# Second attention of a two-layer network: score operands in 32-row strips, stacked by TensorE

## What is computed

```
q = rope((x @ Wqa @ Wqb).reshape(b, s, 16, 8))        # 16 heads of 8
k, v = (x @ Wkva @ Wkvb).reshape(b, s, 4, 8, 2)       # 4 groups of heads share k and v
k = rope(k)
scores = einsum('bqhd,bkhd->bhqk', q, k) * 8**-0.5    # causal mask, then softmax
out = einsum('bhqk,bkhd->bqhd', softmax(scores), v) @ Wout + bout
```

## Time and profile before

| | us |
|---|---|
| three runs | 1310.79, 1312.22, 2832.59 |
| median | 1312.22 |
| span of the profiled execution | 1317.5 |
| PE, DVE, ACT busy in it | 1166.7, 1046.4, 776.6 |

### The profile page before, as it was taken

The page is one execution under the profiler, slowest core; times in us unless marked ns, Lnnn a source line. Parts: engine busy times, 40 slices in busy tenths (PEclk is TensorE's granted clock), DMA queues, the critical chain, the costliest instruction groups (busy, mean ns, idle before and its releaser), DMA issues.

```text
span 1317.5 us, 17710 instructions
## 1 busy us (share of the span) xinstructions
PE 1166.7 (89%) x6249; PEld 680.9 (52%) x6249; DVE 1046.4 (79%) x2018; ACT 776.6 (59%) x1151; POOL 43.9 (3%) x45
## 2 busy tenths in 40 slices
PE   3888647999999855779999999999998799999998
PEld 2333333666666512345444443443332688888886
DVE  4699998788888883879899889888851688888885
ACT  1635414899999710135555656566676566666664
POOL 0000020000000040140000000000000000000000
PEclk9898767899999956589999999999999699999999
DMA  5000000000000214551000000000000121111001
GB/s 161 0 0 1 0 24 17 16 17 16 18 14 1 78 35 79 72 78 16 2 2 2 1 1 2 1 1 1 1 1 1 45 102 56 56 56 56 0 1 33
DMA packets 38169, 35.02 MB, mean 27 GB/s; under 512 B 15162, under 2 KB 33530, under 8 KB 36810
## 3 DMA queue, kind: packets, MB, share of 16 engines
q1 hardware_dynamic: 36082, 31.12, 9.0%
q0 software_dynamic: 2016, 2.96, 1.7%
HBM read 30.85 MB, written 3.08 MB: 26 GB/s over the span
## 4 chain that ended last, share of the span: by engine, by line
PE 61%; DVE 26%; ACT 6%; issue 3%; DMA 3%; SPq 1%; DVEq 0%; ACTq 0%
PE ps L822 10%; PE ps L823 10%; PE ps L824 10%; PE ps L983 9%; DVE arena_a L1766 7%; PE ps L927 7%; PE ps L971 6%; DVE arena_b L1472 3%; DVE mv L1377 2%; PE ps L839 1%; ACT arena_b L1222 1%; DMA arena_a<-q_parts 1%; PE ps L693 1%; DMA arena_a<-arena_a 1%; DVE xn L1384 1%
## 5 line engine op out<-in xcount | busy, mean ns | idle before, releaser
L1766 DVE TENSOR_REDUCE arena_a<-ps 128x1 f32<-128x512 f32 (+3 forms) x560 | 344.4, 668 | 73.2 <-PE ps L931 46.3
L1289 ACT ACTIVATE arena_b<-ps 128x1024 f32<-128x1024 f32 (+3 forms) x320 | 274.0, 894 | 191.8 <-PE ps L971 169.6
L822 PE MATMUL ps<-parts 128*128 128x512 f32 x640 | 273.2, 427 | 7.1 <-DVE parts L1688 4.2
L823 PE MATMUL ps<-parts 128*128 128x512 f32 x640 | 251.5, 393 | 0.0
L824 PE MATMUL ps<-parts 128*128 128x512 f32 x640 | 251.2, 392 | 0.0
L927 PE MATMUL ps<-arena_b,arena_a 128*128 128x512 bf16 (+3 forms) x576 | 190.4, 354 | 6.3 <-DVE arena_a L1766 4.9
L971 PE MATMUL ps<-arena_a,arena_b 128*128 128x512 bf16 (+3 forms) x576 | 163.2, 348 | 0.7 <-ACT arena_b L1289 0.3
L983 PE MATMUL ps<-arena_b 128*32 128x512 f32 (+3 forms) x1280 | 151.1, 544 | 2.5 <-DVE arena_b L1754 2.2
L822 PEld LDWEIGHTS ps<-parts 128*128 128x128 f32 x640 | 122.0, 191 | 36.8 <-DVE parts L1688 9.7
L824 PEld LDWEIGHTS ps<-parts 128*128 128x128 f32 x640 | 121.0, 189 | 26.4
L823 PEld LDWEIGHTS ps<-parts 128*128 128x128 f32 x640 | 121.4, 190 | 22.4
(11 more groups left out here) (274 smaller groups left out, 1445.3 us busy)
## 6 DMA issues: line engine op xcount, KB each, us to landing
arena_b<-expert_weights SPq DMA_DIRECT2D x7, 1024.0 KB, 6.7
arena_a<-q_parts SPq DMA_DIRECT2D x18, 128.0 KB
arena_a<-q_parts POOLq DMA_DIRECT2D x18, 128.0 KB, 5.9
wslot<-in_L_ffn_up_w SPq DMA_DIRECT2D x8, 256.0 KB, 3.1
wslot<-in_L_ffn_down_w SPq DMA_DIRECT2D x8, 256.0 KB, 3.3
wslot<-in_L_ffn_w_gate SPq DMA_DIRECT2D x8, 256.0 KB, 2.9
wslot<-in_L_ffn_w_up SPq DMA_DIRECT2D x8, 256.0 KB, 3.4
wslot<-in_L_ffn_w_down SPq DMA_DIRECT2D x8, 256.0 KB, 3.8
```

What stands on the lines that cost most here:

```text
L822: mm(bank, w(0), x(0), start=start, stop=False)
L823: mm(bank, w(0), x(1), start=False, stop=False)
L1289: a(probs[:, s % 2, 2 * pair:2 * pair + 2, off:CW], ps[:, 2 + 2 * pair:4 + 2 * pair, off:CW], ACT.Exp, scale=scale).then_inc(p2_exp, 1)
L1766: v.tensor_reduce(mx[:, n % 2, i:i + fit, t % TPC, u], b[:, 0:fit * w].rearrange("p (h k) -> p h k", k=w), AX_X, ALU.max)\
```

## The change

The parts of q and k become two fp32r parts each instead of three bfloat16 ones. One head takes KROWS = 24 rows (three pairs of parts of 8 features) and two rows for the maximum, and lies in its own strip of 32 rows; `qst` and `kst` hold the four heads of a group in the four strips, `kst` with the same k in each. A score product contracts 24 rows (slots) or 26 rows (steps) of one strip, where it contracted 128 rows.

- The strips are filled by PE: matmuls with 0/1 matrices `spread` (1 MB, loaded by DMA during the routing, copied to fp32r by POOL) take the parts to their rows (`stack_q`, `stack_k`, 32 units of two products), and ACT copies each bank to `qst` or `kst`, for k with a per-partition bias that puts the ones in place. The DRAM tensors, `stack` and both long memsets are gone.
- Wqa @ Wqb and Wkva @ Wkvb are multiplied once, ahead of the expert layer of layer 0 (two transposes, two products, four ACT copies); `queries`, `keys` and `values_all` then start from the normalized x. k of chunk c is computed into its own 32 rows of banks 6 and 7, so rope and split of k are done once for all chunks (`rope_k`); they need their own rope table `ropek`.
- Slots: a chunk's diagonal blocks of one head go into one bank ("diag", four products of 128 columns and one mask product of 512), the blocks below them into two more ("below3", "below12"). An item has 12 such slots where it had 11; all slots are 616 where they were 600, over the same columns. Slots 0 to 24 run ahead of step 0, after all of q, with `stack_k` of chunks 1 to 3 between them.
- `copy_out` moves from DVE to ACT. The reordering copies of the weights and the addition of the output bias move from DVE to POOL.
- The maximum rows are float32 and go to one strip row of each head.

```diff
-    fit = max(1, CW // ((t % TPC + 1) * P)) if u == t // TPC else 1
-    scores += [("scores", n, t, u, i, fit) for i in range(0, HPG, fit)]
+blocks = [("scores", t, u) for t in range(TPC * c, TPC * c + TPC) for u in range(c)]
+blocks += [("diag", 0, 0), ("below3", 0, 0), ("below12", 0, 0)]
+for k, (what, t, u) in enumerate(blocks):
+    scores += [(what, n, t, u, i) for i in range(HPG)]
     if k == 0 and n > 0:
...
     nc.gpsimd.memset(vaug[:, :, :, HD:HD + 1], 1.0).then_inc(vzero, 1)
...
-        stack(pool, c)
...
+    pool.wait_ge(comb_ready, 2)
+    pool.wait_ge(ld_e, 16)
+    g.tensor_copy(spread, eraw).then_inc(spread_ready, 1)
+    pool.wait_ge(ln_xn, 3 * NC)
+    pool.wait_ge(wo1_ready, 1)
+    g.tensor_tensor(xt[:, :, :], xt[:, :, :], bo1[:, :].unsqueeze(1).broadcast_to([P, NT, D]), ALU.add)\
+        .then_inc(bias_ready, 1)
...
+    nc.tensor.transpose(ps[0:QL, 2, 0:P], wqa[:, :], ident[:, :])
+    nc.tensor.transpose(ps[0:KVL, 3, 0:P], wkva[:, :], ident[:, :]).then_inc(wt_tr, 1)
+    pe.wait_ge(wt_ready, 2)
+    pe.wait_ge(wk_ready, 6)
+    mm(ps[:, 2, 0:2 * D], wqaT[:, :], wqb.rearrange("p a d -> p (a d)"), start=True, stop=True)
+    mm(ps[:, 3, 0:3 * G1 * HD], wkvaT[:, :], wkk.rearrange("p a d -> p (a d)"), start=True, stop=True)\
+        .then_inc(wm_mm, 1)
+    pe.wait_ge(wm_ready, 2)
     for c in range(NC):
...
+    def queries(c):
...
+        pe.wait_ge(ln_h, 2 * NC + c + 1)
...
+        if c >= 2:
+            pe.wait_ge(rope_done, 2 * (c - 1))
+        b = 4 - 2 * (c % 2)
+        mm(ps[:, b, :], wq[:, 0, :], rhs(c), start=True, stop=True)
+        mm(ps[:, b + 1, :], wq[:, 1, :], rhs(c), start=True, stop=True).then_inc(q_mm, 1)
...
+    def keys(c):
...
         pe.wait_ge(ln_h, 2 * NC + c + 1)
...
-            last = mm(ps[:, 2, k * 32:(k + 1) * 32], latk[0:KVL, c % 2, k * P:(k + 1) * P], wkk[:, 2, :],
+        mm(ps[32 * c:32 * c + 32, 6, :], wkv[:, 0, :], rhs(c), start=True, stop=True,
+           tile_position=(0, 32 * c))
+        mm(ps[32 * c:32 * c + 32, 7, :], wkv[:, 1, :], rhs(c), start=True, stop=True,
...
+    def values_all():
+        pe.wait_ge(rope_done, 6)
+        for t in range(NT):
+            last = mm(ps[:, 4, t * 32:(t + 1) * 32], hT[:, PAD + t * P:PAD + (t + 1) * P], wkv[:, 2, :],
                       start=True, stop=True)
...
+    def stack_q(c):
+        pe.wait_ge(split_ready, c + 1)
+        if c == 0:
...
+            e = c * G1 + g
+            if e >= 2:
+                pe.wait_ge(stack_ready, e - 1)
+            mm(ps[:, e % 2, :], spread[:, 0, g, 0, :], q2[:, c % 2, 0, :], start=True, stop=False)
+            mm(ps[:, e % 2, :], spread[:, 0, g, 1, :], q2[:, c % 2, 1, :], start=False, stop=True)\
+                .then_inc(stack_mm, 1)
+    def stack_k(c):
...
+        r = slice(32 * c, 32 * c + 32)
+        for g in range(G1):
+            e = NSTACK + c * G1 + g
+            pe.wait_ge(stack_ready, e - 1)
+            mm(ps[:, 2 + e % 2, :], spread[r, 1, g, 0, :], k2[r, 0, :], start=True, stop=False)
+            mm(ps[:, 2 + e % 2, :], spread[r, 1, g, 1, :], k2[r, 1, :], start=False, stop=True)\
+                .then_inc(stack_mm, 1)
...
+                pe.wait_ge(stack_ready, NSTACK + G1 * (c + 1))
...
+            def pairs(at_, tq, k0, kw, stop=True):
+                return mm(b[:, at_:at_ + kw], qst[r, g, tq * P:(tq + 1) * P], kst[r, g, k0:k0 + kw],
+                          start=True, stop=stop, skip_group_check=not stop)
+            if what[0] == "scores":
+                last = pairs(0, t, u * CW, CW)
+            elif what[0] == "below3":
+                last = pairs(0, TPC * c + 3, c * CW, 3 * P)
+            elif what[0] == "below12":
+                pairs(0, TPC * c + 1, c * CW, P)
+                last = pairs(P, TPC * c + 2, c * CW, 2 * P)
+            else:
+                for k in range(TPC):
+                    pairs(k * P, TPC * c + k, c * CW + k * P, P, stop=False)
+                last = mm(b, identb[:, :], maskqk[:, :].unsqueeze(1).broadcast_to([P, TPC, P]),
+                          start=False, stop=True, skip_group_check=True)
         elif what[0] == "maxima":
             pe.wait_ge(nm_ready, what[1] + 1)
-            last = nc.tensor.transpose(b[0:2 * HPG * TPC, 0:P // 2].bitcast(BF16),
...
+            r = slice(32 * i, 32 * i + MROWS)
+            k = kst[r, g, j * P:(j + 1) * P]
+            q = qst[r, g, chunk(c)]
...
+    keys(NC - 1)
+    queries(2)
+    stack_q(0)
+    queries(3)
+    stack_q(1)
+    stack_q(2)
+    values_all()
+    stack_q(3)
+    stack_k(0)
+    for k, what in enumerate(SLOTS[0]):
         slot(what)
-    latents(NC - 1)
-    heads(NC - 1)
-    for what in FIRST[1]:
-        slot(what)
-    pe.wait_ge(v_ready, NC)
...
+    pe.wait_ge(v_ready, 1)
+    pe.wait_ge(stack_ready, 2 * NSTACK)
     for s, (n, j) in enumerate(STEPS):
...
+        if e < NSTACK:
+            a(qst[:, g, chunk(c)], ps[:, e % 2, :], ACT.Copy).then_inc(stack_ready, 1)
+        else:
+            a(kst[:, g, chunk(c)], ps[:, 2 + e % 2, :], ACT.Identity, bias=onerow[:, :])\
+                .then_inc(stack_ready, 1)
+    norm(2)
...
+        stack_copy(e)
+    act.wait_ge(v_mm, 1)
...
+    def copy_out(n, steps):
...
+        act.wait_ge(pv_mm, steps)
+        if n >= 2:
+            act.wait_ge(slot_read, READ["out", n - 2])
+        a(oT[:, n % 2, :], ps[:, 6, :], ACT.Copy).then_inc(o_copy, 1)
...
+    def rope_q(c):
...
+        b, bank = c % 2, 4 - 2 * (c % 2)
+        dve.wait_ge(q_mm, c + 1)
+        v.tensor_tensor(ra[:, b, :], ps[:, bank, :], ropec[:, chunk(c)], ALU.mult).then_inc(rope_done, 1)
+        v.tensor_tensor(rb[:, b, :], ps[:, bank + 1, :], ropes[:, chunk(c)], ALU.mult).then_inc(rope_done, 1)
+        dve.wait_ge(rope_done, 2 * c + 2)
+        chain(v.tensor_tensor(ra[:, b, :], ra[:, b, :], rb[:, b, :], ALU.add))
         if c >= 2:
-            dve.wait_ge(st_qk[b], 32 * (c // 2))
-        step(v.tensor_copy(q3[:, b, 0, :], ra[:, b, :]))
-        step(v.tensor_copy(k3[0:KR, b, 0, :], rk[0:KR, b, :]))
-        settle()
-        step(v.tensor_tensor(ra[:, b, :], ra[:, b, :], q3[:, b, 0, :], ALU.subtract))
-        step(v.tensor_tensor(rk[0:KR, b, :], rk[0:KR, b, :], k3[0:KR, b, 0, :], ALU.subtract))
-        settle()
-        step(v.tensor_copy(q3[:, b, 1, :], ra[:, b, :]))
-        step(v.tensor_copy(k3[0:KR, b, 1, :], rk[0:KR, b, :]))
-        settle()
-        v.tensor_tensor(q3[:, b, 2, :], ra[:, b, :], q3[:, b, 1, :], ALU.subtract).then_inc(split_ready, 1)
-        v.tensor_tensor(k3[0:KR, b, 2, :], rk[0:KR, b, :], k3[0:KR, b, 1, :], ALU.subtract)\
+            dve.wait_ge(stack_mm, G1 * (c - 1))
+        chain(v.tensor_copy(q2[:, b, 0, :], ra[:, b, :]))
+        v.tensor_tensor(q2[:, b, 1, :], ra[:, b, :], q2[:, b, 0, :].bitcast(F32), ALU.subtract)\
             .then_inc(split_ready, 1)
...
+    def rope_k():
...
+        dve.wait_ge(k_mm, NC)
+        dve.wait_ge(split_ready, NC)
+        v.tensor_tensor(ra[:, 0, :], ps[:, 6, :], ropek[:, 0, :], ALU.mult).then_inc(krope_done, 1)
+        v.tensor_tensor(rb[:, 0, :], ps[:, 7, :], ropek[:, 1, :], ALU.mult).then_inc(krope_done, 1)
+        dve.wait_ge(krope_done, 2)
+        chain(v.tensor_tensor(ra[:, 0, :], ra[:, 0, :], rb[:, 0, :], ALU.add))
+        chain(v.tensor_copy(k2[:, 0, :], ra[:, 0, :]))
+        v.tensor_tensor(k2[:, 1, :], ra[:, 0, :], k2[:, 0, :].bitcast(F32), ALU.subtract)\
+            .then_inc(ksplit_ready, 1)
```

337 lines of the change are left out of this document (146 added, 191 removed).

## The result

The changed kernel takes 1573.22 us (median of four runs, 1567.79 to 1575.96), the kernel before 1313.01 beside it: a ratio of 1.1985, 95% interval 1.1923 to 1.2047. The forecast of 1256 and its whole range lie on the other side. The profiled execution has a span of 1574.2 us, 256.7 more than before. Three marks in the trace split that: the first slot comes at 492.37 (before 523.90), the first exponential at 526.7 (before 558.1), the last one at 1268.7 (before 1011.0). So everything up to the first exponential gained 31.4 us, the stretch of the steps grew from 452.9 to 742.0 us, 289.1 more, and the rest gained 1.0: -31.4 + 289.1 - 1.0 = 256.7.

A forecast was written before the change was run, and what follows sets the result against it. PE was taken to bound the dense attention, DVE 10% behind, after a sparse, low-clock stretch. Terms -4 +1 -20 -17 -24 -6 -7 +19 +2 = -56 gave a span of 1261.5, forecast 1256 us; 8 in 10 from 1222 to 1290.

The forecast's parts named there:

- -4 +1: Routing and merged weights: removing the first memset saves 4 us; POOL's copy of `spread` may hold DVE, costing 1.
- Preparation -20: From 464.8 us to the first slot: 39 us instead of 59.1, with a third of PE's work at half clock.
- The first slots were to bring -8: First slot to first exponential: 25 slots at some 0.75 us and twelve stack units, 26 us instead of 34.
- -9: First two items: 25 us instead of 34.4, as SP and POOL no longer stand before the maxima rows.
- +19: Diagonal steps: eight more changes of array shape at 0.1 us, partly covered, +0.3 us for each of 64 steps.
- +40: Upper bound of the diagonal steps' cost, at 0.15 us a change of array shape.
- -24 -6: Off-diagonal steps: strips overlap and DVE bounds, -0.33 us in 72 four-slot steps (-24); ACT bounds three-slot steps (-6).
- the loss of cover: Steps: prediction is wrong if DVE, alone at its limit, loses its two filled banks while PE is in the values.
- Rival 2: Score products: strips do not overlap, each product waits as now; 1283 us, chance 0.12.
- Rival 3: Short fp32r products in slots and masked steps run at float32's rate, 107 us more: 1363 us; 0.08 including all above 1300.
- Rival 1: Steps: strips overlap, shape changes cost nothing, DVE becomes the bound everywhere; 1231 us, chance 0.22.
- rival 4: Preparation stays at half clock and POOL's work collides with DVE's, +20 +4: 1280 us, chance 0.09.

The follow-up runs named there:

- whole_rows: Changed kernel with every score product contracting all 128 rows instead of one strip (numbers no longer the network's): 1329.32 us.
- fill_probe: Products alone, without the network: two or three strips by turns, off-diagonal and diagonal step patterns, other fills; diagonal step 5.8 us in strips, 3.6 in the whole array.
- entry_probe: Products alone: off-diagonal steps without waits, entered at 1.2 GHz, come to 1.66 us each; also diagonal steps without masks, 1.73 us each.
- paced_probe: No network, but the changed kernel's step loop with its real waits and two slot banks: off-diagonal steps 4.75 us each after the clock falls.
- no_masks: Changed kernel without any mask product, in slots and steps (attention not causal there): 1398.9 us.
- clock_probe: Kernel of its own, PE alone running eleven streams of matmuls in strips and whole array: four strips by turns 0.056 us a product, whole array 0.23.
- strips_grouped: pool_cut with the first slot of a step moved behind the scores of heads 2 and 3, so four strip products stand together: 1426.7 us.
- pool_cut: Changed kernel without mask products on PE; POOL multiplies the exponentials of the diagonal block by zeros and ones: 1397.2 us.

## Why the prediction was wrong

*Ahead of the first exponential the sum was right, by luck.* The terms -4 +1 -20 -8 make -31, and -31.4 was measured, but two of them were too careful and the last did not come. Forecast -4 +1 for the routing: the first transposes stand at 220.66 instead of 228.55, and the first product of the preparation at 457.28 instead of 464.79, -7.5; the tiny operation beside the first memset, 5.65 before, lasts 0.53. Preparation -20: 457.28 to 492.37 is 35.1 instead of 59.1, -24, since it ran at 0.94 of the clock from 461 us on and not at half for a third of it. The first slots were to bring -8 and brought nothing: 34.3 us instead of 34.2, at a clock of 0.50. Timeline of PE, the first of them:

```profile
492.37 1.11 PE L958 MATMUL ps<-parts 24*128 24x128 f32 x4 [0.78 <-ACT parts L1319]
493.41 0.61 PE L971 MATMUL ps<-maskqk,identb 128*128 128x512 bf16 x1
493.95 1.11 PE L958 MATMUL ps<-parts 24*128 24x128 f32 x4
```

A "diag" slot takes 1.58 where 0.75 was forecast; at 2.4 GHz it is still 0.91 (816.09 to 817.00). The masks are part of it: without them the first exponential comes at 518.7. The low clock is not the doing of the score strips here, for whole_rows has it in the same place; what holds it there was not tested. (`stack_k`, in single strips of 32 rows between the slots of both kernels, is one suspect.) The first two items, forecast at -9, took 54.4 us instead of 34.4 (526.67 to 581.08), and 30.8 in whole_rows, so most of that is the strips'.

*The step that failed* is in the parts on the diagonal and off it: both were summed at the clock of the kernel before. "Eight more changes a step at 0.1 are 0.8 ... +19" has two errors. The change was read off the values' column strips, 0.1 to 0.15; between row strips and whole array it is 0.16 to 0.21. That is the small one: +0.1 for 512 changes is some 50 us, near the +40 given as bound. The large one was not in the range: the pattern takes PE to 1.2 GHz, and a diagonal step from 3.6 to 5.8 us (fill_probe). By the experiments, masks in strips cost 174 us in all, their own work included.

*Off the diagonal*, -24 -6 was right in its mechanism, the overlap, and too large even at 2.4 GHz: 2.70 us a step is 0.13 less than before and not 0.33, some -9 instead of -24 for 72 steps. DVE came near the bound but idles 0.21 a step until the first slot product behind the values is there: the loss of cover that the prediction named at its end. Rival 2 falls: strips overlap, 0.225 for four. (The Trainium skill, TensorEngine Tiling (Array Packing), Theoretical Speedup, puts full packing at up to four times, and four products in 0.225 where one takes 0.23 agree with it; TensorE: Matmul & The Clock Gate, Part 3, has 3.07 times, and the measurement here lies above it.) But eight products that kept PE for 1.73 us need 0.45 side by side; they are now held back for DVE one or a few at a time, and the step falls to 1.2 GHz and 4.16 us. That the waits between strip products do this is argued from entry_probe, which has the products without waits and keeps 2.4 GHz, and paced_probe, which has the waits and loses it; in the kernel itself they were not taken out. What the strips cost beyond the masks is some 70 us (no_masks against whole_rows).

*Rival 3*, the only one on the slow side, named a wrong mechanism beside a right one: a short whole-array fp32r product is not at float32's rate but bound by its weight load, 0.112, so 0.057 more than a bfloat16 one, where some 0.10 more (56 / 576) would have eaten the gain. In four strips by turns it is 0.029. But the four of a "diag" slot lie in one strip, one behind the other, and there they take 0.11 each at 2.4 GHz and 0.21 at 1.2 (in the profile four of them last 0.66 and 1.11 us, one 0.32 and 0.47). In whole_rows the form costs 45 us, more than the 31 that the changed kernel gains ahead of its first exponential. *Rival 1* and *rival 4* did not come to pass; POOL's bias addition did hold one DVE operation, 3.53 us instead of 0.69, and was hidden.

*What should have been asked.* The forecast counted the clock as a state of the sparse stage alone. The earlier trace rows had the question in them: at 558 to 593 us PE is busy 28 of 35 at 0.80, in the dense stretch 183 of 185 at 1.00, and the change took most of the work out of the dense stretch and put single-strip products in it. No row of before shows a stream of products in row strips, so the clock of such products was an unknown cost and belonged in the bounds: all steps at half clock would have been a rival: twice PE's 2.1 us for 96 steps off the diagonal and twice 2.95 for 64 on it is 96 x 1.7 + 64 x 2.95 = 352 us more, some 1610.

What stays open: how the 70 us without masks divide between waits and the short diagonal products, what keeps the clock low from 492 to 527 us in the whole array as well, and why strips_grouped is 29 us slower than pool_cut.

## What to carry to other kernels

A PE that is recorded busy can still be at 1.2 GHz: before moving products into strips, ask what fills the array between two changes of shape, and price the stage at both levels of the clock. Four strips side by side in a long stretch do in 0.225 us what takes 0.92 in the whole array (clock_probe); one whole-array product between two strip products (here a mask) costs two changes of some 0.2 us and may cost the clock. When a change bundles a better preparation with a new form of the inner loop, take them apart first: the 31 us ahead of the first exponential were real, though no run here put this preparation ahead of the old steps.
